# Sixteen-head attention and channel mixing over 32 sequences: the second group of row maxima moved to the head of SyncE's step, norm rows made one at a time

## The reference, cut to what matters

```python
x = x + attn(layernorm(x))          # q, k = rope(x Wq), rope(x Wk); v = x Wv; 16 heads of 16
                                    # softmax(q k / 4) v, then Wu and + bu
x = x + ffn(layernorm(x))           # xr, xk = mixes of x with x one token earlier, by mu_r, mu_k
                                    # sigmoid(xr Wr) * (relu(xk Wk)^2 Wv)
```

## Time and profile before

| | |
|---|---|
| median of 3 runs | 2275.34 us (2271.11 to 2275.67) |
| the profiled execution | 2274.27 us, span 2272.4 us |
| mean granted TensorE clock | 0.972 |
| PE / DVE / ACT / POOL busy | 93 / 82 / 72 / 67 % of the span |
| first to last transposed score | 75.0 to 2223.2 us, 2048 of them, 64 in a step |

### The profile page before, as it was taken

One profiled execution on the slowest core, in us unless ns is written; L12 is line 12 of the kernel. 1 busy time (PEld: TensorE's weight loads), 2 busy tenths in 40 slices (PEclk: granted clock), 3 DMA queues, 4 the chain that ended last, 5 costly groups with the idle time before them and its releaser, 6 DMA issues.

```text
span 2272.4 us, 39598 instructions
## 1 busy us (share of the span) xinstructions
PE 2114.4 (93%) x13084; PEld 1085.5 (48%) x13084; DVE 1872.0 (82%) x3598; ACT 1645.5 (72%) x3137; POOL 1514.8 (67%) x1568
## 2 busy tenths in 40 slices
PE   4999999999999999999999999999999999999985
PEld 3445444445454445444444544444445445454433
DVE  5788888878888888888888888888888888888762
ACT  2477777777877777777777777777777777777663
POOL 5347766667866676776676786666777667677335
PEclk8799999999999999999999999999999999999887
DMA  6544455544455553445564445555444556443410
GB/s 153 117 109 106 95 101 120 130 108 106 96 109 111 129 125 99 103 94 110 130 129 110 104 94 110 111 129 120 104 105 95 106 131 130 106 103 88 83 29 23
DMA packets 133467, 242.09 MB, mean 107 GB/s; under 512 B 24849, under 2 KB 79761, under 8 KB 120977
## 3 DMA queue, kind: packets, MB, share of 16 engines
q1 hardware_dynamic: 133264, 239.56, 47.5%
HBM read 136.71 MB, written 83.89 MB: 97 GB/s over the span
## 4 chain that ended last, share of the span: by engine, by line
PE 46%; POOL 18%; issue 15%; ACT 7%; DVE 5%; SPq 5%; DMA 4%; POOLq 0%; ACTq 0%; DVEq 0%
PE d_ps L957 19%; PE st_ps L895 12%; PE pv_ps L927 11%; PE s_ps L913 4%; SPq L314 4%; POOL parts L431 3%; DMA attnT<-attn 3%; DVE mx L707 3%; POOL xrT L440 3%; ACT yn L581 2%; ACT probs L666 2%; POOL f_lo L454 2%; POOL sums L482 2%; POOL rope_t L413 2%; POOL rope_t L416 2%
## 5 line engine op out<-in xcount | busy, mean ns | idle before, releaser
L707 DVE TENSOR_REDUCE mx<-s_ps 128x1 f32<-128x512 f32 x2048 | 1336.6, 678 | 300.9 <-PE s_ps L913 300.5
L666 ACT ACTIVATE probs<-st_ps 128x512 f32<-128x512 f32 x2048 | 1155.7, 597 | 484.9 <-PE st_ps L895 465.5
L895 PE MATMUL st_ps<-q_st,k_st 50*128 50x512 f32 x2048 | 813.3, 461 | 92.3 <-ACT probs L666 50.7
L913 PE MATMUL s_ps<-k_st,q_st 48*128 48x512 f32 x2048 | 815.8, 465 | 7.8 <-DMA k_st<-parts_scratch 5.4
L895 PEld LDWEIGHTS st_ps<-q_st,k_st 50*128 50x128 f32 x2048 | 323.2, 187 | 717.3 <-ACT probs L666 485.1
L927 PE MATMUL pv_ps<-probs,v_ext 128*32 128x512 f32 x4096 | 551.0, 610 | 0.0
L913 PEld LDWEIGHTS s_ps<-k_st,q_st 48*128 48x128 f32 x2048 | 322.6, 187 | 19.1 <-DVE mx L707 10.4
L482 POOL TENSOR_TENSOR sums<-sums,inv 128x256 f32<-128x256 f32 x128 | 93.0, 727 | 305.5 <-DVE inv L734 305.5
L461 POOL TENSOR_TENSOR f_lo<-yn,f_hi 128x512 fp32r<-128x512 f32 x128 | 166.6, 1312 | 44.8 <-ACT f_hi L631 44.7
L927 PEld LDWEIGHTS pv_ps<-probs,v_ext 128*32 128x32 f32 x4096 | 81.1, 108 | 179.1 <-issue 171.3
L431 POOL TENSOR_TENSOR parts<-parts 128x1024 fp32r<-128x1024 f32 x62 | 148.1, 2388 | 19.4 <-ACT parts L596 19.4
(11 more groups left out here) (116 smaller groups left out, 4007.2 us busy)
## 6 DMA issues: line engine op xcount, KB each, us to landing
parts_scratch<-parts SPq DMA_DIRECT2D x64, 1024.0 KB, 4.5
q_st<-parts_scratch SPq DMA_DIRECT2D x128, 256.0 KB, 5.4
k_st<-parts_scratch SPq DMA_DIRECT2D x128, 256.0 KB, 6.3
xn<-in_L_attn_x_dram SPq DMA_DIRECT2D x32, 512.0 KB, 9.2
q_st<-parts_scratch SPq DMA_DIRECT2D x128, 128.0 KB, 6.8
k_st<-parts_scratch SPq DMA_DIRECT2D x128, 128.0 KB, 7.3
attnT<-attn SPq DMA_DIRECT2D x512, 32.0 KB, 2.0
y<-in_L_attn_x_dram SPq DMA_DIRECT2D x32, 512.0 KB, 7.0
```

Source lines behind the costliest of these rows:

```text
L666: nc.scalar.activation(probs[:, u % SLOTS, j, :], st_ps[:, n % 2, :], ACT.Exp, scale=float(D) ** -0.5).then_inc(exp_done, 1)
L707: nc.vector.tensor_reduce(mx[:, col:col + 1], s_ps[:, ring_bank(n), :], AX.X, ALU.max).then_inc(max_done, 1)
L895: nc.tensor.matmul(st_ps[:, n % 2, :], k_st[par][row:row + SROWS + MROWS, slot, c * P:(c + 1) * P], q_st[par][row:row + SROWS + MROWS, slo ...
L913: nc.tensor.matmul(s_ps[:, ring_bank(n), :], q_st[at][row:row + SROWS, slot, qc * P:(qc + 1) * P], k_st[at][row:row + SROWS, slot, :], sta ...
```

## The change

Six things change, and no arithmetic:
- TensorE transposes group 1 of the maxima in unit 1 ahead of V's first half instead of behind it; `JOBS` exchanges the two, and so their banks.
- VectorE splits group 1 after the maxima of (1, 1) and (1, 2) instead of (1, 3) and (2, 0), and does the second `gate_v` at (0, 2) instead of (0, 3).
- SyncE's step begins with `move_max(b, 1)`, ahead of `store_parts` and `move_attn(b-1, 3)`.
- The statistics of the second layernorm come ahead of the transposes of group 0's attention sums on VectorE, for its second half ahead of two maxima, and their scales come ahead of `divide(b, 0)` on GpSimd; `norm2` is made in four single rows at (5, 3), (6, 0), (7, 0), (7, 2) instead of pairs at (6, 0) and (7, 2).
- `norm1`: rows 0 and 1 go to (15, 0) and (15, 2) of the step before, rows 2 and 3 from (2, 0) and (2, 1) to (0, 0) and (0, 2); GpSimd's `scales` for them goes ahead of the second pair of rope products.
- VectorE's `shift(1, 1)` goes from (9, 3) to (10, 0).

```diff
--- before.py
+++ after.py
@@ -172,7 +172,7 @@
...
-        JOBS = [("O", -2, 1, gated, 2, 2), ("V", 1, 0, v_done, 2, 1), ("M", 0, 1, msplit, 8, 4),
+        JOBS = [("O", -2, 1, gated, 2, 2), ("M", 0, 1, msplit, 8, 4), ("V", 1, 0, v_done, 2, 1),
                 ("V", 1, 1, v_done, 2, 2), ("XT", 2, 0, xnT_split, 2, 1), ("XT", 2, 1, xnT_split, 2, 2),
@@ -186,7 +186,7 @@
...
         DENSE = ["O1", "V0", "V1", "XT", "WU0", "WU1", "Q0", "Q1", "YT", "K0", "K1", "FK0", "FK1", "R0", "R1", "O0"]
-        MAX_T = {1: (0, 1), 5: (0, 2), 9: (0, 3), 13: (1, 0)}
+        MAX_T = {5: (0, 2), 9: (0, 3), 13: (1, 0)}
@@ -352,9 +352,9 @@
...
+                move_max(b, 1)
                 store_parts(b.plus(1), 1 - par, 1)
                 move_attn(b.plus(-1), 3)
-                move_max(b, 1)
                 store_out()
@@ -496,9 +496,9 @@
...
                 low_a(1)
+                scales(b.plus(-1), 0, ln2_stat, ln2_scale, yn_done, mv2, rs2, nm2)
                 divide(b, 0)
-                for n in range(2):
-                    scales(b.plus(-1), n, ln2_stat, ln2_scale, yn_done, mv2, rs2, nm2)
+                scales(b.plus(-1), 1, ln2_stat, ln2_scale, yn_done, mv2, rs2, nm2)
@@ -518,9 +518,9 @@
...
                 rope_mults(b.plus(2), 1, 0)
+                scales(b.plus(3), 1, ln1_stat, ln1_scale, xn_done, mv1, rs1, nm1)
                 rope_mults(b.plus(2), 1, 1)
                 rope_sums(b.plus(2), 1)
-                scales(b.plus(3), 1, ln1_stat, ln1_scale, xn_done, mv1, rs1, nm1)
@@ -564,22 +564,20 @@
...
-                def norm1(c):
-                    s = b.plus(2)
+                def norm1(s, c):
                     if s.active():
...
-                def norm2(n):
-                    s = b.plus(-1)
+                def norm2(c):
+                    s, n = b.plus(-1), c // 2
                     if s.active():
...
                             act.wait_ge(f_lo_done, s.plus(-1).count(4, 4))
-                        for c in (2 * n, 2 * n + 1):
-                            nc.scalar.activation(yn[:, c, :], y[1 - par][:, c, :], ACT.Identity, scale=rs2[:, c:c + 1],
-                                                 bias=nm2[:, c:c + 1]).then_inc(yn_done, 1)
+                        nc.scalar.activation(yn[:, c, :], y[1 - par][:, c, :], ACT.Identity, scale=rs2[:, c:c + 1],
+                                             bias=nm2[:, c:c + 1]).then_inc(yn_done, 1)
@@ -640,17 +638,17 @@
...
-                extras = {(0, 0): [(norm1, 0)], (0, 2): [(norm1, 1)],
+                extras = {(0, 0): [(norm1, b.plus(2), 2)], (0, 2): [(norm1, b.plus(2), 3)],
                           (1, 2): [(high_a, 0)], (1, 3): [(v_evac, 0)],
-                          (2, 0): [(norm1, 2)], (2, 1): [(norm1, 3)], (2, 3): [(v_evac, 1)],
+                          (2, 3): [(v_evac, 1)],
                           (3, 1): [(high_a, 1)], (3, 2): [(xT_evac, 0)], (3, 3): [(xT_evac, 1)],
-                          (6, 0): [(norm2, 0)], (6, 3): [(qk_evac, 0, 0)],
-                          (7, 2): [(norm2, 1)], (7, 3): [(qk_evac, 0, 1)], (8, 2): [(yT_evac, 0)],
+                          (5, 3): [(norm2, 0)], (6, 0): [(norm2, 1)], (6, 3): [(qk_evac, 0, 0)], (7, 0): [(norm2, 2)],
+                          (7, 2): [(norm2, 3)], (7, 3): [(qk_evac, 0, 1)], (8, 2): [(yT_evac, 0)],
                           (8, 3): [(yT_evac, 1)], (9, 3): [(qk_evac, 1, 0)], (10, 0): [(high_f, 0, 0)],
...
                           (12, 3): [(relu, 1)], (13, 1): [(high_f, 1, 0)], (13, 3): [(tanh, 0)],
-                          (14, 0): [(high_f, 1, 1)], (14, 3): [(tanh, 1)]}
+                          (14, 0): [(high_f, 1, 1)], (14, 3): [(tanh, 1)], (15, 0): [(norm1, b.plus(3), 0)], (15, 2): [(norm1, b.plus(3), 1)]}
                 if first(b.plus(2)):
@@ -830,17 +828,17 @@
...
-                extras = {(0, 0): [(gate_v, b.plus(-2), 0)], (0, 3): [(gate_v, b.plus(-2), 1)],
+                extras = {(0, 0): [(gate_v, b.plus(-2), 0)], (0, 2): [(gate_v, b.plus(-2), 1)],
                           (1, 0): [(normalise, prev, 3, 0), (normalise, prev, 3, 1)],
-                          (1, 3): [(normalise, prev, 3, 2), (split_max, b, 1, 0)], (2, 0): [(split_max, b, 1, 1)],
+                          (1, 1): [(split_max, b, 1, 0)], (1, 2): [(split_max, b, 1, 1)], (1, 3): [(normalise, prev, 3, 2)],
                           (3, 3): [(split_xnT, 0)], (4, 0): [(split_xnT, 1)], (4, 3): [(residual, 0)],
-                          (5, 0): [(normalise, b, 0, 0), (stats2_of, 0, 0)], (5, 1): [(stats2_of, 0, 1), (normalise, b, 0, 1)],
-                          (5, 2): [(residual, 1)], (5, 3): [(split_max, b, 2, 0)], (6, 0): [(split_max, b, 2, 1)],
-                          (6, 1): [(stats2_of, 1, 0)], (6, 2): [(stats2_of, 1, 1)],
+                          (5, 0): [(stats2_of, 0, 0), (stats2_of, 0, 1)], (5, 1): [(normalise, b, 0, 0), (normalise, b, 0, 1)],
+                          (5, 2): [(residual, 1)], (5, 3): [(split_max, b, 2, 0), (stats2_of, 1, 0)],
+                          (6, 0): [(split_max, b, 2, 1), (stats2_of, 1, 1)],
                           (7, 1): [(normalise, b, 0, 2)],
...
                           (9, 0): [(normalise, b, 1, 0)], (9, 1): [(normalise, b, 1, 1)],
-                          (9, 2): [(split_max, b, 3, 0), (shift, 1, 0)], (9, 3): [(split_max, b, 3, 1), (shift, 1, 1)],
+                          (9, 2): [(split_max, b, 3, 0), (shift, 1, 0)], (9, 3): [(split_max, b, 3, 1)], (10, 0): [(shift, 1, 1)],
                           (10, 2): [(shift, 0, 0)], (11, 1): [(shift, 0, 1)],
@@ -1014,6 +1012,8 @@
...
                         if j == 1:
+                            if u == 1:
+                                row_max_T(b, 1)
                             dense(u, 0)
```

## The result

| | before | after |
|---|---|---|
| median | 2273.23 us | 2341.06 us (2336.92 to 2342.29) |
| ratio, 95% interval | | 1.0291 (1.0269 to 1.0312) |
| profiled execution, its span | 2274.27, 2272.4 us | 2336.92, 2335.1 us |
| mean granted clock | 0.972 | 0.958 |
| mean of steps 2 to 29 | 67.43 us | 69.60 us |

A forecast was written before the change was run, and what follows sets the result against it. TensorE, 93% busy, was taken to lose time only in its gaps; 31 steps at -0.5 (-16 us) and the clock (+24) took 2274.27 to 2282.3, as a median 2284 us. The 8-in-10 range was 2238 to 2304.

The forecast's parts named there:

- SyncE's order: Maxima's moves first on SyncE: store and attention moves go 1.45 us later, costing +0.8 a step at (4, 1) (0.3 to 1.3).
- The step with a late landing in the trace of before: Step with its store at 885.72: `f_hi` started 6.76 us after it, against 5.19 ordinarily; taken as sample of the late landing.
- The transposes' own move: Unit 1, group 1's transposes ahead of V: 0.1 us a step (-0.1 to 0.7), hidden in the sum.
- `norm1`: Norm rows at (15, 0) and (15, 2): exp of (15, 3) ends later, (0, 1) waits 0.15 us (0 to 0.5).
- the clock term: Half clock after the gaps at (4, 0) and (4, 1) in 25 steps instead of 9: 16 x 1.5 = +24 us (0 to 37).
- `shift(1, 1)` one maximum later is 0: VectorE's shift read by `f_hi` at (10, 1), then Wk in unit 11: no cost, bounds -0.1 and 0.3 us.
- Statistics ahead of the sums: Earlier statistics and single norm rows: (6, 3) gains 0.85 us, (8, 1) gains 0.62, together -1.47 a step.
- The clock falls no oftener: Rival: the late landing costs its 0.8 us but half clock at (4, 0) comes no oftener; 2259 us, chance 0.22.
- the landing is not late: Rival: attention lands on time or nobody needs it then, first gap goes; 2184 us, half the shift 2240, chance 0.14.
- Everything is late: Rival: second split ends after 1021, SyncE waits, clock falls nearly every step, (6, 3) gain lost; 2330 us, chance 0.13.

The follow-up runs named there:

- a_old_sp: The changed kernel with SyncE's old order (store, attention moves, then the maxima's moves): 2294.3 us, ratio 1.0104.
- a_store_last: The changed kernel with SyncE's order maxima's moves, attention moves, then the store: 2260.86 us, ratio 0.9957.
- b_stats: The kernel before with only the second layernorm's edits (VectorE's order in units 5 and 6, scales ahead of divide, single norm2 rows): 2243.61 us, ratio 0.9876.
- b_shift: The kernel before with only VectorE's shift(1, 1) moved from (9, 3) to (10, 0): 2303.85 us, ratio 1.0144.
- b_shift_d: b_shift with shift(0, 0) also moved, from (10, 2) to (10, 3): 2286.51 us, ratio 1.0056.
- b_stats_keep: b_stats, but the transposes of the attention sums stay first at (5, 0), ahead of both statistics: 2235.21 us, ratio 0.984.
- a_alone: The kernel before with only group 1's transposes ahead of V, gate_v, the earlier splits and SyncE's new order: 2339.44 us, ratio 1.0302.
- b_store_last: The kernel before with SyncE's order attention moves, maxima's moves, then the store: 2277.58 us, ratio 1.0038.
- b_best: The kernel before with the edits of b_store_last and b_stats_keep together: 2287.89 us, ratio 1.0067.
- b_x_later: b_best with the load of x moved behind the moves of group 2's maxima on SyncE: 2225.18 us, ratio 0.9799.

## Why the prediction was right in direction and wrong in size

**Right.** *SyncE's order.* The numbers foretold for it came: maxima at 8.2 (8.0 forecast), store at 11.0 (10.8), `f_hi` at 16.25 (16.0), 2 us of waiting on ScalarE in every step, gaps of 1.50 and 0.38, and +0.98 in units 3 and 4 (+0.8). The step with a late landing in the trace of before was a true sample of the changed kernel, and a_old_sp and a_store_last, which bring `f_hi` back to 14.8, show that SyncE's order made it late. The transposes' own move cost nothing that shows (unit 1: -0.10). *Statistics:* -1.00 in unit 6 (-0.85 forecast) and -0.58 in 8 to 10 (-0.62), of which b_stats has 0.49. *`norm1`:* +0.26 in unit 0 (0.15, bounds 0 and 0.5).

The direction was in part luck. The forecast had a quiet step 0.5 shorter and turned the sum to the slower side by the clock term alone (-16 + 24); the measured quiet step is 1.20 longer, for reasons that the sum did not have.

**The step that failed first: the term "`shift(1, 1)` one maximum later is 0", with bounds of -0.1 and 0.3.** It is +1.05, alone 31.5 us. I had looked at who reads the shift (`f_hi` at (10, 1), then Wk in unit 11) and not at what runs beside it. `f_hi(1)` starts 0.6 later (45.21 after (0, 0) in b_shift, 44.62 in before), and that is hidden: the second `f_lo` waits for the first. But GpSimd's two `f_lo`, 2.62 before, take 3.8 (changed kernel, GpSimd and VectorE):

```profile
531.69 3.83 POOL L461 TENSOR_TENSOR f_lo<-yn,f_hi 128x512 fp32r<-128x512 f32 x2 [0.75 <-ACT f_hi L629]
...
531.79 0.73 DVE L793 SCALAR_TENSOR_TENSOR yn<-xrT,mu_sb,ynT 128x512 f32<-128x512 f32 x1
...
533.65 0.73 DVE L793 SCALAR_TENSOR_TENSOR xrT<-xrT,mu_sb,ynT 128x512 f32<-128x512 f32 x1
```

The wait of 0.96 behind it is where the unit's 1.05 went; b_shift has it with this edit alone and b_shift_d halves it by starting one shift 0.6 later. The trace of before already had a shift of 1.22 beside an `f_lo`.

**The second: "Statistics ahead of the sums", which priced who waits for the statistics and not who waits for the transposes that they overtake.** The product with V in unit 5 writes the one bank of `pv_ps`, which VectorE must have read; it started 0.55 late, and unit 5 is +0.61. b_stats_keep takes back just that, at 0.33 more in unit 6. The working had asked this of SyncE's queue and not of VectorE's order.

**The clock was mis-sized, in the price of a fall.** 22 steps fell instead of the 25 forecast, 13 more rather than 16, but such a step is 2.34 longer than a quiet one, where I had put 1.5, from "one fall is 3.4 us at half clock". For the nine falls of 3.4 us behind the usual gap of 1.5 that was right: they cost 1.42 each. In the other 13 one or both of two things came on top. In ten the half clock lasted 6.8 us (the two of these with the usual gap cost 2.67), and the trace of before had one such among its nine, which the working passed over. In 11 the gap at (4, 0) was 1.62 to 3.08, mean 2.44, where the landing was later still; eight of the ten are among these. Clock term: +30 instead of +24.

Forecast for a quiet step -0.5, measured +1.20. The difference, 1.7: shift 1.05, `pv_ps` 0.61, units 3 and 4 0.18, unit 0 0.11, less 0.15 in unit 6 and 0.13 in units 1 and 2.

**The rivals.** "The clock falls no oftener" and "the landing is not late" are refuted by the 22 falls and by `f_hi` at 16.25. "Everything is late" had the time nearly right (2330) and much of the clock, but the wrong mechanism for the steps: the second split was in time and units 6 to 10 kept their gain. (Its parts added up, the chances are 0.36 for faster and 0.18 for the same, not 0.37 and 0.17.) The range was too narrow since it carried the doubt on landing and clock but gave the edit called free a bound of 0.3 a step.

**Open:** why the clock fell in 30 of 30 steps of a_alone and in 22 after: of the steps with gaps of 1.5 and 0.4, all 19 fell in the one and 11 of 19 in the other. No run changed the second gap alone.

## What to carry to other kernels

When an instruction is moved in an engine's order, look at who reads its result, at what it overtakes or lets pass (here a bank of `pv_ps`), and at what now runs beside it on the other of VectorE and GpSimd: two moves that the sum had at nothing were 1.7 us of a 67 us step. In a single DMA queue a large transfer that nobody awaits soon goes behind the small ones that somebody does; but look first at what waits for the large one to land, here the stacks, x behind them and group 2's maxima behind x. With the store alone moved nothing was won (b_store_last, 2277.58); with the load of x behind the maxima, its readers moved to suit, and the statistics of b_stats_keep (35 of the 70 us, by itself) it was 2196.83. The reordering was not run without the statistics. A trace of before that has one unlucky step of the changed kernel's kind was here a good forecast of it: its gaps came out within a tenth.

## What the runs showed of the hardware

- **VectorE and GpSimd hold each other up.** A shift of 0.73 beside an `f_lo` of 1.3 makes the latter 1.9 (after, b_shift), or the `f_lo` makes the shift 1.2 (before, b_shift_d); beside maxima alone `f_lo` stays at 1.3; 3.82 for the pair falls to 3.22 when the second shift starts 0.60 behind its `f_lo` instead of 0.01 (b_shift_d, b_shift). The Trainium skill, "SBUF — State Buffer", "SBUF: two separate sides", says that VectorE with two SBUF inputs and a GpSimd operation that reads SBUF share a pair of ports which is locked for a whole instruction by the one that starts first. The durations agree. The recorded starts do not decide who was first: `f_lo` stands 0.10 ahead of the shift (531.69, 531.79) and was still the one to be lengthened.
- **Small moves behind a large transfer land late.** With the 1 MB store issued 0.42 ahead of them it is 4.8 us from the issue of the attention moves to `f_hi`, with the store behind them 3.85, although four moves of maxima (2.7 us of queue) go ahead in both of after and a_store_last. The same with x: group 2's maxima, issued at 27.1 in both, landed at 34.8 behind its load (b_best) and at 32.1 ahead of it (b_x_later).
- **The half clock after short gaps.** Gaps of 1.46 to 1.53 at (4, 0), nearly all followed by a second of about 0.4, brought the lower level (1.2 GHz) in 11 of 19 steps of the changed kernel and in 19 of 19 of a_alone; gaps of 1.62 and more in all 11 steps of either. A gap of 1.31 to 1.35 in a_old_sp brought it in 1 of 17, and that one had a second of 0.39 behind it. Over the nine kernels that have a gap there in every step (before, after, a_alone, a_old_sp and five of `b_`, 270 steps) it is looser. Of single gaps, none of 123 up to 1.45 brought a fall, and 55 of 69 above did; one of 2.52 in a_old_sp did not. Of gaps with a second of 0.1 to 0.4 behind them, 10 of 16 did up to 1.45, 30 of 38 from 1.46 to 1.58, and all 24 above. So a short second gap seems to count, and the length of the first does not decide by itself.
